# Tile norms' last steps and feed-forward rounding on GpSimd behind its divisions, and one reciprocal placed behind the copies in two of eight steps

## What is computed

```python
x = x + L0_xattn(ctx, ctx, layernorm(x), mask)
x = x + L0_attn(layernorm(x))
x = x + L0_ffn(layernorm(x))
x = x + L1_xattn(layernorm(x), ctx, ctx)
x = x + L1_attn(layernorm(x))      # causal softmax attention, 16 heads of 16
x = x + L1_ffn(layernorm(x))       # inputs and weights rounded to FP4 in blocks of 16
```

## Time and profile before

| | us |
|---|---|
| median of 3 runs | 1418.12 |
| the profiled execution | 1421.31 |
| its span, first to last instruction | 1418.0 |
| TensorE busy, matmuls (91% of the span) | 1294.1 |
| TensorE busy, weight loads | 899.6 |
| VectorE busy | 976.0 |
| ScalarE busy | 802.0 |
| GpSimd busy | 690.7 |

### The profile page before, as it was taken

The page is one execution under the profiler, slowest core; times in us unless marked ns, Lnnn a source line. Parts: engine busy times, 40 slices in busy tenths (PEclk is TensorE's granted clock), DMA queues, the critical chain, the costliest instruction groups (busy, mean ns, idle before and its releaser), DMA issues. The chain is left out here.

```text
span 1418.0 us, 28592 instructions
## 1 busy us (share of the span) xinstructions
PE 1294.1 (91%) x11120; PEld 899.6 (63%) x11122; DVE 976.0 (69%) x1876; ACT 802.0 (57%) x1373; POOL 690.7 (49%) x383
## 2 busy tenths in 40 slices
PE   6999999999999988988789999998998988888887
PEld 3666666667667665546456676666665676666564
DVE  4685776766666654856777767688766879776674
ACT  4766666666666655536456656556465645565431
POOL 2856656566666542310146654444445455544333
PEclk9999999999999999999999999999899989999999
DMA  5312112112113030007330210020010121000000
GB/s 164 101 51 66 46 46 67 46 60 76 46 46 113 2 113 1 1 5 219 106 93 31 60 52 31 31 61 31 31 51 31 44 61 47 31 2 1 5 9 18
DMA packets 30533, 74.23 MB, mean 52 GB/s; under 512 B 4033, under 2 KB 16193, under 8 KB 26177
## 3 DMA queue, kind: packets, MB, share of 16 engines
q1 hardware_dynamic: 30400, 72.41, 16.8%
HBM read 65.06 MB, written 7.34 MB: 51 GB/s over the span
## 5 line engine op out<-in xcount | busy, mean ns | idle before, releaser
L655 POOL TENSOR_TENSOR ca_prob<-ca_prob,ca_inv_sum 128x1024 f32<-128x1024 f32 x256 | 493.6, 1935 | 448.5 <-DVE ca_inv_sum L892 448.4
L732 PEld LDWEIGHTS bank<-ident,ca_prob 128*128 128x128 f32 x2048 | 240.9, 143 | 102.5 <-issue 75.2
L732 PE MATMUL bank<-ident,ca_prob 128*128 128x128 f32 x2048 | 273.7, 278 | 29.2 <-DVE ca_v L841 25.4
L856 DVE CUSTOM_DVE_ANT_0 ca_neg_logit<-bank,ca_mask_add 128x1024 f32<-128x1024 f32 x128 | 151.6, 1221 | 103.7 <-PE bank L722 76.6
L802 ACT ACTIVATE ca_prob<-bank,ca_neg_max 128x1024 f32<-128x1024 f32 x128 | 142.3, 1113 | 110.7 <-DVE ca_neg_max L859 110.5
L859 DVE TENSOR_REDUCE ca_neg_max<-bank 128x1 f32<-128x1024 f32 x128 | 150.5, 1218 | 59.9 <-PE bank L722 59.6
L802 ACT ACTIVATE ca_prob<-ca_neg_logit,ca_neg_max 128x1024 f32<-128x1024 f32 x128 | 146.9, 1149 | 68.3 <-DVE ca_neg_max L856 68.3
L869 DVE COPY ca_probT<-bank 128x512 f32<-128x512 f32 x256 | 163.7, 681 | 7.0 <-PE bank L732 7.0
L813 ACT ACTIVATE ca_probT<-bank 128x512 f32<-128x512 f32 x256 | 139.6, 594 | 50.8 <-PE bank L732 48.5
L722 PE MATMUL bank<-ca_kT,ca_q_blk 32*128 32x512 f32 x1024 | 150.3, 657 | 4.5 <-DVE ca_v L841 2.7
L749 PEld LDWEIGHTS bank<-ca_probT,ca_v 128*32 128x32 f32 x4096 | 111.8, 113 | 55.7 <-issue 42.4
(11 more groups left out here) (281 smaller groups left out, 1712.2 us busy)
## 6 DMA issues: line engine op xcount, KB each, us to landing
ca_ctxT<-in_ctxT SPq DMA_DIRECT2D x16, 1024.0 KB, 5.3
ctxT<-in_ctxT SPq DMA_DIRECT2D x16, 1024.0 KB, 4.8
ca_mask_i<-in_mask SPq DMA_DIRECT2D x32, 256.0 KB, 6.1
ek_ctxT<-in_ctxT SPq DMA_DIRECT2D x12, 512.0 KB, 5.3
early_k<-ek_out SPq DMA_DIRECT2D x48, 128.0 KB, 3.4
ca_kT<-early_k SPq DMA_DIRECT2D x12, 512.0 KB, 5.7
lat<-in_x SPq DMA_DIRECT2D x1, 1024.0 KB, 4.8
out<-lat SPq DMA_DIRECT2D x8, 128.0 KB, 1.9
```

Of the source, the lines that this page charges most:

```text
L655: pool.tensor_tensor(self.prob[:, x, :], self.prob[:, x, :], self.inv_sum[:, x:x + 1].broadcast_to([P, CTX]), ALU.mult).then_inc(self.norm ...
L732: tr = pe.transpose(self.core.bank[:, x, n * P:(n + 1) * P], self.prob[:, 2 * (s % 2) + p, (4 * h + n) * P:(4 * h + n + 1) * P], self.core ...
L856: dve.tensor_tensor_reduce(self.neg_logit[:, p, :], scores, self.mask_add[:, b % 2, :], -1.0, BIG, ALU.add, ALU.min, self.neg_max[:, y:y + ...
```

## The change

On VectorE the norm of a tile is cut in two. `inverse_on_vector` keeps the reciprocal of the root; the rest, one step of Newton's method on it and the subtraction and product over 256 columns, is `finish_on_pool`, six instructions on GpSimd, behind the divisions and the attention's own work of the step (lag 2 for the causal input, 13 for the feed-forward input). Tile 7 of the causal part and tiles 6 and 7 of the feed-forward part keep `finish_on_vector`.

Of the rounding of the feed-forward input VectorE keeps the maximum, scale and reciprocal of a block (`scale_x`, lag 14) and the exponent mask (step 4, lag 15). GpSimd does the product (lag 14), steps 5 to 7 (lag 15) and steps 8 and 9 (lag 16). The product and sum of one `scalar_tensor_tensor` become two instructions (n = 6 and 7), which makes ten steps in all; `divide_x` and `round_x` go. The transposes of the rounded input and their copy move from lag 16 to lag 17.

In the steps with s % 8 of 4 and 7 the reciprocal of half 0 stands behind VectorE's value copy and transposed copies. After the loop, tile 5 is treated likewise, its copies stand ahead of the first hidden tile, and TensorE multiplies by the values before the first gate projection.

```diff
@@ class TileNorm @@
     def stats_on_vector(self, dve, t):
+        wait(dve, self.xn_ready, t)
...
-    def finish_on_vector(self, dve, t):
+    def inverse_on_vector(self, dve, t):
         dve.wait_ge(self.std_ready, t + 1)
         dve.reciprocal(self.rstd[:, :], self.std[:, :]).then_inc(self.fix_step, 1)
-        dve.wait_ge(self.fix_step, 4 * t + 1)
-        dve.scalar_tensor_tensor(self.fix[:, :], self.rstd[:, :], self.rstd[:, 0:1], self.var[:, :], ALU.mult,
-                                 ALU.mult).then_inc(self.fix_step, 1)
...
+    def finish_on_pool(self, pool, t):
+        lat, wide = self.core.lat[:, t, :], [P, D]
+        pool.wait_ge(self.fix_step, 6 * t + 1)
+        pool.tensor_tensor(self.fix[:, :], self.rstd[:, :], self.rstd[:, :], ALU.mult).then_inc(self.fix_step, 1)
+        pool.wait_ge(self.fix_step, 6 * t + 2)
+        pool.tensor_tensor(self.fix[:, :], self.fix[:, :], self.var[:, :], ALU.mult).then_inc(self.fix_step, 1)
+        pool.wait_ge(self.fix_step, 6 * t + 3)
+        pool.tensor_scalar(self.fix[:, :], self.fix[:, :], -0.5, 1.5, ALU.mult, ALU.add).then_inc(self.fix_step, 1)
+        pool.wait_ge(self.fix_step, 6 * t + 4)
+        pool.tensor_tensor(self.rstd[:, :], self.rstd[:, :], self.fix[:, :], ALU.mult).then_inc(self.fix_step, 1)
+        pool.wait_ge(self.fix_step, 6 * t + 5)
+        pool.tensor_tensor(self.xn[:, :], lat, self.mv[:, 0:1].broadcast_to(wide), ALU.subtract).then_inc(self.fix_step, 1)
+        pool.wait_ge(self.fix_step, 6 * t + 6)
+        pool.tensor_tensor(self.xn[:, :], self.xn[:, :], self.rstd[:, 0:1].broadcast_to(wide), ALU.mult)\
+            .then_inc(self.xn_ready, 1)
+
+    def finish_on_vector(self, dve, t):
+        dve.wait_ge(self.fix_step, 6 * t + 1)
+        dve.tensor_tensor(self.fix[:, :], self.rstd[:, :], self.rstd[:, :], ALU.mult).then_inc(self.fix_step, 1)
+        dve.wait_ge(self.fix_step, 6 * t + 2)
+        dve.tensor_tensor(self.fix[:, :], self.fix[:, :], self.var[:, :], ALU.mult).then_inc(self.fix_step, 1)
...
@@ class Fp4Tiles @@
+    def x_step_on(self, eng, t, first, last):
+
+        x, e = self.x[:, :], self.xe
+        steps = fp4_steps(x, DB, self.xmag[:, :], self.xscale[:, :], self.xinv[:, :], x, e)
+        grid, scale = fp4_scaled(x, self.xscale[:, :], DB)
+        for n in range(first, last):
+            wait(eng, self.x_step, 9 * t + n)
+            if n < 6:
+                steps[n](eng).then_inc(self.x_step, 1)
+            elif n == 6:
+                eng.tensor_scalar(x, x, 1.0 - 2.0**-24, None, ALU.mult).then_inc(self.x_step, 1)
+            elif n == 7:
+                eng.tensor_tensor(x, x, e, ALU.add).then_inc(self.x_step, 1)
+            elif n == 8:
+                steps[7](eng).then_inc(self.x_step, 1)
+            else:
+                eng.tensor_tensor(grid, grid, scale, ALU.mult).then_inc(self.x_ready, 1)
+
+    def scale_x(self, dve, t, xn_ready):
         dve.wait_ge(xn_ready, t + 1)
...
+        self.x_step_on(dve, t, 0, 3)
@@ TensorE @@
-                for t in tile_at(s, 16):
+                for t in tile_at(s, 17):
                     ff.latent_transposes(pe, t)
...
+            ca.times_v(pe, 30)
             ff.project(pe, 0, 0)
-            ca.times_v(pe, 30)
@@ GpSimd @@
+                for t in tile_at(s, 2):
+                    causal_input(t)
+                for t in tile_at(s, 13):
+                    feed_forward_input(t)
+                for t in tile_at(s, 14):
+                    ff.x_step_on(pool, t, 3, 4)
+                for t in tile_at(s, 15):
+                    ff.x_step_on(pool, t, 5, 8)
+                for t in tile_at(s, 16):
+                    ff.x_step_on(pool, t, 8, 10)
...
-            both(0)
+            ff.divide_hidden(pool, 0)
+            ff.x_step_on(pool, 5, 3, 4)
+            ff.scale_hidden(pool, 0)
             both(1)
+            ff.x_step_on(pool, 5, 5, 10)
@@ VectorE @@
                 ca.maxima(dve, s)
-                ca.inverse(dve, s, 0)
+                if s % 8 not in (4, 7):
+                    ca.inverse(dve, s, 0)
...
                 if s >= 1:
                     ca.take_t_on_vector(dve, s - 1, 0)
+                if s % 8 in (4, 7):
+                    ca.inverse(dve, s, 0)
                 ca.inverse(dve, s, 1)
...
                 for t in tile_at(s, 2):
-                    causal_input(t)
+                    norm1.inverse_on_vector(dve, t)
+                for t in tile_at(s, 13):
+                    norm2.inverse_on_vector(dve, t)
...
                 for t in tile_at(s, 14):
-                    feed_forward_input(t)
+                    ff.scale_x(dve, t, norm2.xn_ready)
                 for t in tile_at(s, 15):
-                    ff.round_x(dve, t)
+                    ff.x_step_on(dve, t, 4, 5)
...
             ca.take_pv(dve, 30)
-            feed_forward_input(5)
+            ff.scale_x(dve, 5, norm2.xn_ready)
+            ca.take_t_on_vector(dve, STEPS - 1, 0)
             ff.hidden(dve, 0)
-            ff.round_x(dve, 5)
-            ca.take_t_on_vector(dve, STEPS - 1, 0)
             ff.round_hidden(dve, 0)
             ca.take_pv(dve, 31)
+            ff.x_step_on(dve, 5, 4, 5)
```

More of the change, by code:

```diff
@@ L2278, in _, with causal_input, feed_forward_input @@
             ca.add_output_bias(pool)
+            def causal_input(t):
+                if t >= 1:
+                    banks.wait_filled(pool, ("sx", t - 1))
+                norm1.finish_on_pool(pool, t)
+            def feed_forward_input(t):
+                ff.x_free(pool, t)
+                norm2.finish_on_pool(pool, t)
             for s in range(STEPS):
@@ L2443, in _ @@
             ff.round_hidden(dve, 1)
-            causal_input(7)
+            norm1.inverse_on_vector(dve, 7)
+            banks.wait_filled(dve, ("sx", 6))
+            norm1.finish_on_vector(dve, 7)
             ff.hidden(dve, 2)
@@ L2455, in _ @@
             ff.hidden(dve, 4)
[L2456 removed]
+            ff.x_step_on(dve, 6, 4, 10)
             sa.divide(dve, 7)
```

40 lines of the change are left out of this document (11 added, 29 removed).

## The result

The changed kernel takes 1373.2 us in the median of four runs (1370.4 to 1374.2), the kernel before 1417.0 beside it (1411.2 to 1420.8). The ratio is 0.969, with an interval of 0.965 to 0.973: 44 us, 3.1%, where 1376 was forecast. The profiled execution took 1374.2 us and has a span of 1371.8; before's took 1421.3 at a granted clock of 0.965, where other executions of the same kernel had 0.964 to 0.975 and 1410.9 to 1422.3 us, so the two traces differ by 47.1 us and the medians by 44.

What follows compares the result with a forecast made beforehand. It took TensorE's idle time behind a VectorE late at certain points, and the half clock that follows, as the bound. Terms 12.2 + 7.5 + 5.3 + 12 + 4 = 41, some 42 with small things, gave 1376 us; range 1352 to 1405.

Steps and rivals of the forecast that it cites:

- Feed-forward input: Steps 24 to 56: norm and division off VectorE start the maxima earlier, removing five TensorE stalls; 12.2 us gained.
- Rounding: Steps 25 to 57: feed-forward rounding off VectorE; no TensorE stall put down to it, so 0 counted.
- Causal norm: Steps 12 to 60: norm on GpSimd frees VectorE, with a new 1.9 us TensorE wait; 7.5 us gained over seven tiles.
- D: GpSimd's time for the causal norm's last steps, six instructions with pauses: 2.4 us, bounded by 2.0 and 4.7.
- Reciprocal: Remainders 4 and 7: moving it behind VectorE's copies loses nothing and shortens stalls ahead of the causal scores; 5.3 us gained.
- The clock: In the loop, about 36 us at half clock go with the idle time, at 40% each; 12 us taken.
- After the loop: Tile 5's copies ahead of the hidden tile remove TensorE's stall before the last product by values; 4.0 us net.
- VectorE's busy time: Sign to look for: about 60 us less in the loop, with the 1.9 us one-number instructions gone.
- Half given back: Rival: ScalarE's exponentials and key copies also hold banks and the clock still falls; 22 us gained, 1396; chance 0.22.
- GpSimd's norm too late: Rival: small GpSimd instructions cost far more than the fit, stalling TensorE in seven tiles; slower, 1431; chance 0.11.
- Nothing comes of it: Rival: the shared operand path's wait changes sides, GpSimd's divisions grow as VectorE's small instructions shrink; 1418; chance 0.04.
- More: Rival: the waits left in the forecast go too, with all their half clock; 60 us gained, 1358; chance 0.03.

Runs made afterwards that it cites:

- u3: Changed kernel with norm, division and rounding of the feed-forward input of tiles 0 to 4 back on VectorE: 1392.0 us.
- s3: Kernel before with only the feed-forward input of tiles 0 to 4 on GpSimd, VectorE's remaining norms in four-instruction form: 1403.2 us.
- u2: Changed kernel with the causal norm's last steps back on VectorE in the loop, in four-instruction form: 1393.8 us.
- v2: Changed kernel with the causal norm's last steps back on VectorE in the loop, its one-number operations reading per-partition scalars: 1358.4 us.
- u1: Changed kernel with the reciprocal of half 0 back ahead of the copies in all steps: 1388.3 us.
- s1: Kernel before with only the reciprocal of half 0 moved behind the copies in remainders 4 and 7: 1411.9 us.
- w1: Changed kernel with the causal norm back on VectorE and the reciprocal behind the copies in remainder 7 alone: 1391.0 us.
- d1: Changed kernel with three more wide subtractions in GpSimd's causal norm, making it 2.07 us longer: 1386.8 us.
- u4: Changed kernel with the old order behind the loop and tile 5's input on VectorE again: 1376.6 us.
- s2: Kernel before with only the causal norm's last steps on GpSimd in the loop, VectorE's remaining norms in four-instruction form: 1412.5 us.

## Why the prediction was right, step by step

The total was right to 3 us in the medians, 1376 against 1373.2; against the profiled execution, from which it was worked out, to 5 (1379 against 1374.2). The idle time was right part by part; the clock's term was too small by nearly half, and that the total still came so close is partly luck.

- *Feed-forward input, 12.2 us.* Right. The twelve stalls of 24.4 us shrank to three of 3.5, under the 6 foreseen, TensorE's idle time in remainders 0 and 1 fell by 12.0 us (17.3 to 5.3), and putting the part back brings 13.1 us (u3).
- *Rounding, 0.* No run tested it by itself, and no wait of TensorE of over 0.6 us names GpSimd's rounding. But remainder 3, to which the transposes of the rounded input moved, has 1.5 us more idle time (3.1 to 4.6); it goes in u3, where they are back in remainder 2, and is there in s3 (4.7). The prediction put this move at nothing.
- *Causal norm, 7.5 us.* The idle time in remainders 4 and 5 fell by 7.8 us (17.7 to 9.9). D was right to 0.1 us, the new wait 8.0 us in four tiles instead of 1.9 in each of five, and u2's idle time is 10.3 us more with a form that waits twice. What was missing is an alternative: the step moved was expensive because of VectorE's form, and v2 shows that the move itself is not needed.
- *Reciprocal, 5.3 us.* Right for the idle time: 5.4 us less in remainder 7 (13.4 to 8.0), and 5.0 us in all in u1 and in s1. That it loses nothing holds only while the causal norm is not on VectorE (s1, w1: 2.6 to 2.8 us in remainders 4 and 5).
- *The clock, 12 us.* The term that was mis-sized: 21.6 us of TensorE's busy time. The time at 1.2 GHz fell by 44 us, not 36, and each of these cost 0.49 us, not 0.40. The two traces overstate it a little, since before's is of an execution with a low clock (3 us is what they differ by more than the medians), but it stays well above 12. The prediction gave each part its share of the clock; the parts alone gave 10.7 us of busy time and together 21.6, so here the shares could not be added.
- *After the loop, 4.0 us.* 2.4 in the stretches, of which 1.4 are idle time; u2 and d1 differ there by 3.0 and 1.9 us from the changed kernel with the same code, so 2.4 is no sharp number. The 4.04 us ahead of L749 are gone, but three waits behind it grew by 1.0, 0.2 and 0.5 us and a new one of 0.6 stands ahead of L759; the prediction had 0.7 at most. u4 puts the whole edit at 3.4.
- *The sum*: 23.5 idle where 25.0 were written, 21.6 clock where 12, 2.4 behind the loop where 4.0, 1.3 lost ahead of the loop where 0. In the traces that is 46.2 us for the 41 that were added up: the clock gave 9.6 us more than written, the rest 4.4 less.
- *VectorE's busy time* was to fall by about 60 us in the loop and fell by 47.9. Of the missing 12 us 7.4 are one instruction, L174 on 16 numbers a partition: five times 1.65 us in the loop, where it took 0.18 before. VectorE's timeline of step 24 (as rows 3), then GpSimd's:

```profile
919.08 1.65 DVE L174 TENSOR_SCALAR ca_ff_xscale<-ca_ff_xmag 128x16 f32<-128x16 f32 x1
...
921.27 2.36 DVE L859 TENSOR_REDUCE ca_neg_max<-bank 128x1 f32<-128x1024 f32 x2 [0.25 <-PE bank L722]
...
918.81 1.89 POOL L655 TENSOR_TENSOR ca_prob<-ca_prob,ca_inv_sum 128x1024 f32<-128x1024 f32 x1 [1.25 <-DVE ca_inv_sum L892]
```

  With the norm gone, L174 comes where L1712 was, and waits for the division in its stead. It costs nothing, since the maxima wait for their scores anyway (0.25 us idle). Another 3.4 us are two instructions of the feed-forward weights that now meet GpSimd (L178 in step 25, L180 in step 49, 1.7 us each), as the prediction said.
- *Rivals.* Half given back, 1396: no; less idle time did bring the clock up. GpSimd's norm too late, 1431: a small instruction takes 0.19 us; its price of 7 x d is confirmed by d1 (6.6 x d, for 2.07 us more), but the clock cost 0.4 us a tile and not 2.7, so D would have had to reach an estimated 2.4 + 42 / 7 - 0.4 = 8.0 and not 5.7 us. Nothing comes of it: the divisions did not grow (1935 ns on average before and after). More, 1358: v2 reaches that time, by its own way.

The 6 us that the prediction would have lost with a GpSimd of half VectorE's speed were not lost: the wide steps took 0.61 us on GpSimd against 0.41 to 0.43 on VectorE, and D was 2.4, not 3.3. The advice of the Trainium skill to keep such work on VectorE (GPSIMD Engine Reference, section "4.1 Engine selection") still held, for another reason than GpSimd's speed: v2.

Partly open: why remainder 7 grows by 3.7 us when only the causal norm moves (s2), and by 4.8 in u1 with its stalls unchanged. In both 3.1 us of it are one step, 55 (its length, busy times and clock in the kernel before, then in s2, as rows 1):

```profile
1222.52:1231.93 9.41, 7.44 (x72) 5.86 (x76) 6.87 (x10) 6.46 (x11) 7.33 (x5) 1.00 0.01 2
```

```profile
1211.48:1224.01 12.53, 10.55 (x74) 8.17 (x78) 6.89 (x10) 6.66 (x11) 7.32 (x5) 0.73 0.01 2
```

The idle time is 2.0 us in each, before the same instruction, but 6.8 us at 1.2 GHz follow it in s2 and in u1 and none in the kernel before. There a stall of 2.8 us two steps earlier, behind VectorE's causal norm, had been followed by 3.4 us at 1.2 GHz; with the norm on GpSimd that stall and its slow time are gone. Whether the one shifts the other, or single executions differ by as much, was not tried.

## What to carry to other kernels

When an instruction on one number takes 1.9 us, look whether it ends where another engine's instruction ends, and try another form of it before moving it: here two calls were worth 17 us on the kernel before, and made the move to GpSimd unnecessary. Size idle time part by part, since it nearly added here, but the clock for all parts together: here the same part was worth more busy time as the last stalls taken away than as the first (the reciprocal 11.1 us in u1, 2.3 in s1). A norm on a second engine is late by that engine's queue (3.7 us of divisions here) before it is late by its own 2.4 us.
